# Rotated attention: masking by GpSimd after the exponential, values in every other slot, one query and key product

## The reference, cut to what matters

```
x = wide attention(x)                       # 16 heads of 64
x = causal attention with slopes(x)         # then a mixture of experts
x = rotated attention(x)                    # this one; then a mixture of experts
x = grouped attention(x), recurrence, grouped attention

q = (x @ Wqa @ Wqb).reshape(b, s, 16, 8)    # rotated attention
kv = (x @ Wkva @ Wkvb).reshape(b, s, 4, 8, 2)
q, k = rope(q), rope(k)                     # r1 = x1*cos - x2*sin, r2 = x1*sin + x2*cos
scores = q k^T * 8**-0.5, causal            # -inf above the diagonal
out = softmax(scores) @ v @ Wout + bout
```

## Time and profile before

| quantity | value |
|---|---|
| median of 3 runs | 2320.3 us |
| the profiled execution, its own time | 2318.05 us |
| its span, first to last instruction | 2316.3 us |
| rotated attention, first to last `score` | 1388.6 to 1606.5 us |
| PE busy over the span | 88% |
| DVE, ACT, POOL busy over the span | 67%, 52%, 36% |
| mean granted TensorE clock | 0.933 |

### The profile page before, as it was taken

The page is one execution under the profiler, slowest core; times in us unless marked ns, Lnnn a source line. Parts: engine busy times, 40 slices in busy tenths (PEclk is TensorE's granted clock), DMA queues, the critical chain, the costliest instruction groups (busy, mean ns, idle before and its releaser), DMA issues. The chain is left out here.

```text
span 2316.3 us, 52936 instructions
## 1 busy us (share of the span) xinstructions
PE 2046.8 (88%) x20735; PEld 1381.6 (60%) x20735; DVE 1544.5 (67%) x2742; ACT 1199.4 (52%) x2044; POOL 826.4 (36%) x1272
## 2 busy tenths in 40 slices
PE   5999999999969997999779989997599995479996
PEld 3666666666657895566569976664355543335553
DVE  4777778787754444677354447775689875768993
ACT  3444444444343333666723326665478776447774
POOL 4444444444425341333044514441233323423330
PEclk9999999999969997999789999999699997669998
DMA  5000000000000021444000204441234420124441
GB/s 169 1 1 1 1 1 1 1 1 1 2 0 7 5 56 44 121 121 115 3 4 1 56 16 118 122 117 33 71 102 116 116 61 1 43 79 110 116 110 45
DMA packets 157124, 120.99 MB, mean 52 GB/s; under 512 B 13856, under 2 KB 129456, under 8 KB 156884
## 3 DMA queue, kind: packets, MB, share of 16 engines
q1 hardware_dynamic: 156884, 117.65, 18.8%
HBM read 63.48 MB, written 54.12 MB: 51 GB/s over the span
## 5 line engine op out<-in xcount | busy, mean ns | idle before, releaser
L911 DVE TENSOR_REDUCE l_group_mx<-maxima 128x4 f32<-128x1024 f32 x248 | 303.9, 1226 | 58.8 <-PE maxima L704 57.3
L839 ACT ACTIVATE l_group_pr<-scores 128x1024 f32<-128x1024 f32 x256 | 261.7, 1022 | 72.0 <-PE scores L725 69.4
L2176 POOL TENSOR_TENSOR l_wide_tiles_sum<-l_wide_pr 128x256 f32<-128x256 f32 x256 | 180.9, 728 | 212.2 <-ACT l_wide_pr L2119 212.2
L2147 DVE RECIPROCAL l_wide_rc<-bank 128x256 f32<-128x256 f32 x128 | 223.9, 1749 | 8.4 <-PE bank L2080 7.9
L2119 ACT ACTIVATE l_wide_pr<-scores 128x512 f32<-128x512 f32 x256 | 139.0, 595 | 163.1 <-PE scores L2063 163.1
L2131 DVE TENSOR_REDUCE l_wide_mx<-maxima 128x2 f32<-128x512 f32 x248 | 159.4, 685 | 52.9 <-PE maxima L2043 52.5
L2109 ACT ACTIVATE l_wide_qk<-bank 128x512 f32<-128x512 f32 x128 | 76.5, 597 | 175.6 <-PE bank L2030 175.6
L911 DVE TENSOR_REDUCE l_slope_mx<-maxima 128x6 f32<-128x768 f32 x124 | 118.9, 959 | 64.9 <-PE maxima L711 63.3
L911 DVE TENSOR_REDUCE l_rope_mx<-maxima 128x6 f32<-128x768 f32 x124 | 118.8, 958 | 44.0 <-PE maxima L711 43.0
L839 ACT ACTIVATE l_slope_pr<-scores 128x768 f32<-128x768 f32 x128 | 103.6, 810 | 77.6 <-PE scores L732 77.4
L745 PE MATMUL bank<-l_group_pr,va 128*32 128x256 f32 x2048 | 143.4, 399 | 0.0
(11 more groups left out here) (468 smaller groups left out, 4852.3 us busy)
## 6 DMA issues: line engine op xcount, KB each, us to landing
l_group_st<-stack_dram SPq DMA_DIRECT2D x128, 192.0 KB, 3.8
l_slope_st<-stack_dram SPq DMA_DIRECT2D x64, 192.0 KB, 3.8
l_rope_st<-stack_dram SPq DMA_DIRECT2D x64, 192.0 KB, 3.9
stack_dram<-l_group_parts SPq DMA_DIRECT2D x64, 192.0 KB, 2.3
stack_dram<-l_group_parts SPq DMA_DIRECT2D x64, 128.0 KB, 1.9
stack_dram<-l_slope_parts SPq DMA_DIRECT2D x32, 192.0 KB, 2.4
stack_dram<-l_rope_parts SPq DMA_DIRECT2D x32, 192.0 KB, 2.3
stack_dram<-l_slope_parts SPq DMA_DIRECT2D x32, 128.0 KB, 2.2
```

The costliest lines, as they stand in the source:

```text
L839: act.activation(pr[:, i % AHEAD, :, 0:keys], Tp[:, :, 0:keys], ACT.Exp).then_inc(s["exps"], 1)
L911: dve.tensor_reduce(mx[:, b % 2, :, :, i], max_bank(i, b)[:, :, 0:BLOCKS * keys].rearrange("p z (a k) -> p z a k", k=keys), AX.X, ALU.max, ...
L2147: own.done(dve.reciprocal(rc[:], Ob[i % 2][:, S:2 * S]))
L2176: pool.tensor_tensor(tiles_sum[:, i % 2, z, :], pr[:, i % 2, z, 0:S], pr[:, i % 2, z, S:2 * S], ALU.add).then_inc(s["added"], 1)
```

## The change

Only "rope" computes differently; of the other kinds one table entry is written in another form.

1. The corner matmuls of `score` (L732) are left out for "rope". Instead POOL zeroes the exponentials above the diagonal in place with one `affine_select` per pair, a new piece `cut`. `value i` waits for the cuts of its two pairs, no longer for the exponentials.
2. `swapped` is gone, with its weights. `by_sin` is made from the same product as `by_cos`: DVE reads partitions 64 to 127 and writes 0 to 63, and the other way round, in two instructions of 64 partitions. The sine table is exchanged to match.
3. `parts` is divided into three pieces, with a `cut` between them. In "slope" and "group" the three stand one behind the other, as before.
4. The slots of "rope" are set anew on all engines. `value` stands in slots 1, 3, 5 and 7 of PE (before 1, 2, 5, 6), `qk` in slot 2 together with `v`, `turnmax` in slot 4 (before 3). `max` is one slot later against `score`.

```diff
     "rope": {
         "pe": [
-            [("score", 2, 0), ("max", 7, 1), ("qk", 0, 3), ("value", 0, 0)],
+            [("score", 2, 0), ("max", 6, 1), ("qk", 0, 3), ("v", 0, 2)],
...
         "pool": [
-            [("split", 0, 1)],
-            [("parts", 0, 3)],
+            [("split", 0, 1), ("cut", 3, 0), ("parts", 0, 3)],
+            [("cut", 4, 0), ("parts", 1, 3)],
...
     "rope": {
-        "pe": [("norm", 0, 0), ("norm", 0, 1), ("qk", 0, 0), ("swapped", 0, 0), ("qk", 0, 1), ("swapped", 0, 1), ("v", 0, 0), ("v", 0, 1)],
+        "pe": [("norm", 0, 0), ("norm", 0, 1), ("qk", 0, 0), ("qk", 0, 1), ("v", 0, 0), ("v", 0, 1)],
...
-                if causal:
+                if kind == "slope":
                     for half in range(2):
...
-                pe.wait_ge(s["exps"], PAIRS * b + 2 * i + 2)
+                pe.wait_ge(s["cut"] if kind == "rope" else s["exps"], PAIRS * b + 2 * i + 2)
...
-                dve.tensor_tensor(by_cos[:], bank[:].rearrange("p (a s) -> p a s", a=2),
-                                  angles[:, 0, :].unsqueeze(1).to_broadcast([P, 2, S]), ALU.mult).then_inc(drained[m], 1)
-            elif what == "swapped":
-                if b == 0:
-                    dve.wait_ge(s["set_act"], 2)
-                wait(dve, s["summed"], b)
-                dve.tensor_tensor(by_sin[:], bank[:].rearrange("p (a s) -> p a s", a=2),
-                                  angles[:, 1, :].unsqueeze(1).to_broadcast([P, 2, S]), ALU.mult).then_inc(drained[m], 1)
+                both = bank[:].rearrange("p (a s) -> p a s", a=2)
+                dve.tensor_tensor(by_cos[:], both, angles[:, 0, :].unsqueeze(1).to_broadcast([P, 2, S]), ALU.mult)
+                for z in range(2):
+
+                    mine, other = slice(64 * z, 64 * z + 64), slice(64 * (1 - z), 64 * (1 - z) + 64)
+                    ins = dve.tensor_tensor(by_sin[mine], both[other], angles[other, 1, :].unsqueeze(1).to_broadcast([64, 2, S]), ALU.mult)
+                ins.then_inc(drained[m], 1)
...
+            elif what == "cut":
+                pool.wait_ge(s["exps"], PAIRS * b + i + 1)
+                own_tiles = pr[:, i % AHEAD].rearrange("p z (t q) -> p z t q", q=S)[:, :, :, 0:P]
+                pool.affine_select(out=own_tiles, in_=own_tiles, compare_op=ALU.is_ge, fill=0.0, base=0,
+                                   pattern=[[0, 2], [0, NT], [1, P]], channel_multiplier=-1).then_inc(s["cut"], 1)
```

More of the change, by code:

```diff
@@ L251 @@
     "slope": {"norm": 1, "qk": 0, "turnmax": 0, "turn1": 1, "v": 0, "turn0": 0},
-    "rope": {"norm": 1, "qk": 0, "swapped": 1, "turnmax": 0, "turn1": 1, "attn": 1, "v": 0, "project": 1, "turn0": 0},
+    "rope": {"turn0": 0, "project": 1, "qk": 0, "v": 1, "turn1": 0, "turnmax": 1, "attn": 0, "norm": 1},
     "group": {"norm": 0, "qk": 1, "turnmax": 1, "turn1": 0, "reg_scores": 1, "attn": 0, "v": 1, "project": 1, "reg_turn": 0, "turn0": 1, "reg_value": 0},
@@ L309 @@
         "pe": [
-            [("score", 0, 0), ("max", 5, 1), ("swapped", 0, 3)],
-            [("score", 1, 0), ("max", 6, 1), ("value", 3, -1)],
-            [("score", 2, 0), ("max", 7, 1), ("qk", 0, 3), ("value", 0, 0)],
-            [("score", 3, 0), ("max", 0, 2), ("turn1", 0, -1), ("turnmax", 0, 1)],
-            [("score", 4, 0), ("max", 1, 2), ("v", 0, 2), ("attn", 0, -1)],
-            [("score", 5, 0), ("max", 2, 2), ("value", 1, 0)],
-            [("score", 6, 0), ("max", 3, 2), ("project", 0, -1), ("value", 2, 0)],
@@ L317 @@
-            [("score", 7, 0), ("max", 4, 2), ("turn0", 0, 0), ("norm", 0, 4)],
+            [("score", 0, 0), ("max", 4, 1), ("turn0", 0, -1), ("project", 0, -2)],
+            [("score", 1, 0), ("max", 5, 1), ("value", 3, -1)],
+            [("score", 2, 0), ("max", 6, 1), ("qk", 0, 3), ("v", 0, 2)],
+            [("score", 3, 0), ("max", 7, 1), ("value", 0, 0)],
+            [("score", 4, 0), ("max", 0, 2), ("turn1", 0, -1), ("turnmax", 0, 1)],
+            [("score", 5, 0), ("max", 1, 2), ("value", 1, 0)],
@@ L318 @@
+            [("score", 6, 0), ("max", 2, 2), ("attn", 0, -1), ("norm", 0, 4)],
+            [("score", 7, 0), ("max", 3, 2), ("value", 2, 0)],
         ],
         "act": [
-            [("norm", 0, 3), ("score", 0, 0)],
-            [("score", 1, 0), ("xn", 0, 4)],
+            [("score", 0, 0)],
+            [("score", 1, 0)],
             [("take", 1, -1), ("score", 2, 0)],
-            [("score", 3, 0)],
-            [("score", 4, 0)],
-            [("attn", 0, -1), ("score", 5, 0)],
-            [("take", 0, 0), ("v", 0, 2), ("score", 6, 0)],
@@ L327 @@
-            [("score", 7, 0)],
+            [("score", 3, 0), ("v", 0, 2)],
+            [("score", 4, 0), ("xn", 0, 5)],
+            [("score", 5, 0)],
+            [("take", 0, 0), ("score", 6, 0)],
+            [("score", 7, 0), ("attn", 0, -1), ("norm", 0, 4)],
         ],
         "dve": [
-            [("turn0", 0, -1), ("max", 5, 1)],
-            [("swapped", 0, 3), ("max", 6, 1)],
-            [("max", 7, 1), ("join", 0, 1), ("qk", 0, 3)],
-            [("max", 0, 2)],
+            [("max", 4, 1)],
@@ L334 @@
+            [("turn0", 0, -1), ("project", 0, -2), ("max", 5, 1)],
+            [("max", 6, 1)],
+            [("qk", 0, 3), ("max", 7, 1)],
+            [("join", 0, 1), ("max", 0, 2)],
             [("turnmax", 0, 1), ("turn1", 0, -1), ("max", 1, 2)],
             [("max", 2, 2)],
-            [("max", 3, 2), ("project", 0, -1)],
-            [("max", 4, 2)],
+            [("max", 3, 2)],
         ],
         "pool": [
-            [],
-            [],
-            [("split", 0, 1)],
-            [("parts", 0, 3)],
@@ L440 @@
 for _kind in FIRST:
-    FIRST[_kind]["pool"] = [("parts", 0, 0), ("parts", 0, 1)]
+    FIRST[_kind]["pool"] = [("parts", _i, _b) for _b in range(HOSTED) for _i in range(3)]
     FIRST[_kind]["sp"] = [(_what, _i, _b) for _b in range(HOSTED) for _what, _i in (
@@ L551, in bank_of @@
         def bank_of(what, b):
-            early = causal and b < HOSTED and what in ("norm", "qk", "swapped", "v")
+            early = causal and b < HOSTED and what in ("norm", "qk", "v")
             return (Ob if early else Mb)[fill[what, b][0]]
@@ L672, in pe_piece @@
                 ins.then_inc(full[m], 1)
-            elif what in ("qk", "swapped"):
-                if what == "qk" and b == 0:
+            elif what == "qk":
+                if b == 0:
                     pe.wait_ge(s["weights"], 1)
@@ L1082, in host @@
             if what == "first":
-                first(engine, eng)
+                first(engine, eng, 3 if engine == "pool" else 1)
             elif what in ("stat0", "stat1"):
```

63 lines of the change are left out of this document (32 added, 31 removed).

## The result

The changed kernel took 2353.27 us (median of 4 runs, 2351.68 to 2359.26), the kernel before on the same chip 2318.35 (4 runs, 2312.38 to 2320.38): ratio 1.0164, 95% interval 1.0142 to 1.0186. The forecast was 2344, range 2323 to 2368. The profiled span grew from 2316.3 to 2352.3.

A forecast was written before the change was run, and what follows sets the result against it. Waits for DVE's reads and POOL's cuts, not PE, were to bound a batch: 16.0 us for 13.92. Eleven full distances (+23), the ends and -2.1 in the experts gave +26.5, less 1: 2344 us, range 2323 to 2368.

The forecast's parts named there:

- PE stops being the bound: Rotated attention: 2.2 to 2.4 us a batch leave PE, but waits for DVE and POOL make it 16.0 for 13.92.
- Rival 1: Every rope batch: PE stays the bound, DVE's reads hidden, rounds closing in 1.51 us; -29 us, 2289 us; chance 10%.
- DVE's waits: Longer DVE work between reductions starts `max 6` 0.7 us late, `max 0` about 1.0, `turnmax` 0.6.
- The reads: DVE's three reads of the product, 0.61 + 0.61 + 0.62 = 1.84 us in one piece ahead of pair 7's reduction.
- POOL's queue and the cut: Behind `split`, cuts of 0.66 us and pieces of `parts` end at 15.2; `value 2` waits 1.5 us for cut 5.
- Rival 3: POOL's select as dear as a subtraction, 1.16 us a cut: batch 17.8, about 2368 us; chance 12%.
- rival 2: POOL reaches cut 5 early, cuts cost nothing on the path: +0.9 to +1.6 us a batch, 2329 to 2338; chance 17%.
- `spread` half a microsecond behind: The `spread` DMA, behind `high`, is usable at 15.5 us of the 16.0 batch; cheaper cuts win only that half.
- The ends: First `score 0` +0.9 us, first two distances +2.6, last two +0.8, behind the last `score 0` +1.3.
- "11 x 2.1" term: Eleven full distances from `score 0` to `score 0`, each 16.0 us for 13.92, together +23 us.

The follow-up runs named there:

- e2: Changed kernel with the two sine reads of 64 partitions made one of 128, leaving out the exchange of halves; 2342.50 us, ratio 1.0111.
- e9: Kernel before with only the single product and its three reads; corner matmuls kept, no cuts, order and banks of before; 2322.42 us, ratio 1.0034.
- e7: Changed kernel with cut 5 moved ahead of piece 1 of the parts in GpSimd's lists; 2338.57 us, ratio 1.0102.
- e11: Changed kernel with cuts of half the width, the second 64 queries of each diagonal tile left uncut; 2338.19 us, ratio 1.0108.
- e1: Changed kernel without cuts on GpSimd, corner matmuls back in the score, values waiting for the exponentials; 2335.22 us, ratio 1.0078.
- e4: Changed kernel with v and norm moved into PE's waits and repeated three and five times there; 2355.04 us, ratio 1.0169.

## Why the prediction was right, and where its size was off

**PE stops being the bound.** Right: busy 12.35 of 16.36, before 13.92 of 13.92. Rival 1 needed VectorE's reads hidden in the 0.55 us gaps; the waits for L909 are all there.

**DVE's waits.** `max 0` 1.29 late (forecast 1.0), `max 6` 0.53 (0.7), `turnmax` 0.37 (0.6). The reads were the mis-sized term: 2.13 us from 1494.40 to 1496.53, forecast 1.84. The working took 0.61 for a 0.69 us instruction, as the next one starts before the end of the last. For full reads that is right: in e2 they start 0.61 apart. The three of the change start 0.71 apart, so the overlap is lost there. The same happens in e9, which has these reads in another order; only the reads that go from one half of the partitions to the other differ from e2's. The 0.29 is most of the 0.36 us by which the batch at full clock is over 16.0; POOL's queue has 0.13, and small gains go the other way. That a read of 64 partitions costs as much as one of 128 held.

**POOL's queue and the cut.** Right in order, place and size. e7 and e11 show it twice over: moving the cut removes the wait of `value 2`, and shortening it brings PE's waits for cuts from 9.5 us to 1.7. (The forecast's 3.4 us for every 0.08 us of a cut is too much by its own sum: three cuts in eleven batches give 2.6.) Rival 3 (1.16 us a cut) and rival 2 (cuts free) fall with it. Rival 2's own figure of 2329 to 2338 is about where e7 and e11 end, since both take the cut off the path and meet the next wait.

**`spread` half a microsecond behind.** Right, and it needed e1 and e7 to be seen: in both `score 0` waits for it, up to 1.4 and 1.3 us, once the cuts are out of the way.

**The ends.** First `score 0` not late at all (forecast +0.9), and the first two distances +5.4 instead of +2.6. The first distance alone is 17.97 for 15.00, and the clock has a part in it: it was still at its lower level for most of that batch, with a mean of 0.57, where the kernel before had 0.88.

```profile
1385.71:1403.68 17.97, 15.07 (x157) 8.89 (x158) 10.84 (x14) 8.38 (x14) 9.68 (x16) 0.57 0.36 93
```

How large that part is wasn't separated. The tail was 2.0 us shorter than reckoned. These nearly cancel, and that is luck. Each kernel has one profile, and what follows the stage, unchanged in all of them, took between 649 and 657 us from the first `max` of "group" on, so a microsecond or two at the ends can be chance.

**The clock.** The step that failed. The forecast expected the granted clock to stay at 2.4 GHz, because "no idle time is over 1.5 us". (Nor had it survived "waits of 0.2 us only": the kernel before kept 1.00 through waits of 0.6 and 0.4.) It fell in nearly every batch. A batch that lost nothing by it, and two stretches at the lower level in the batch of 17.82:

```profile
1437.80:1454.16 16.36, 13.46 (x191) 9.13 (x188) 11.73 (x20) 8.90 (x15) 11.15 (x19) 0.90 0.37 101
1448.80:1452.30 3.50, 3.50 (x38) 2.11 (x32) 1.98 (x3) 1.77 (x3) 3.37 (x5) 0.51 0.34 97
1471.16:1476.20 5.04, 5.04 (x52) 3.57 (x48) 3.38 (x7) 1.62 (x2) 2.70 (x5) 0.50 0.48 141
1482.90:1486.40 3.50, 3.50 (x43) 2.04 (x42) 1.75 (x5) 1.81 (x3) 3.44 (x5) 0.51 0.14 37
```

```profile
1453.37 0.86 PE L745 MATMUL bank<-l_rope_pr,va 128*32 128x256 f32 x16 [0.68 <-POOL l_rope_pr L1025]
...
1488.19 0.86 PE L745 MATMUL bank<-l_rope_pr,va 128*32 128x256 f32 x16 [0.37 <-POOL l_rope_pr L1025]
```

A mean near 0.50 is the 1.2 GHz level, where the value pair takes 1.51 us for 0.86. What a fall costs depends on where it lies. From 1448.80 and from 1482.90 it lies late in the batch, ahead of `value 2`. POOL's queue doesn't slow down with PE, so `value 2` only waits less, 0.68 and 0.37 us instead of 1.53, and the time of the batch is still set by cut 5: such a fall alone costs nothing (16.36).

A fall that covers the first microseconds of a batch, as from 1471.16, delays the product, the reads and `split`, and so the cuts: `split` starts 1.46 us later into the batch than at full clock (1481.40 against 1497.76), which is the whole of 17.82 against 16.36. A fall over `value 2` itself makes it 17.0.

Seven of the eleven full distances are longer than 16.41 by falls at such places. Eleven at 16.36 would be 26.7 us over before; measured are 34.2, so 7.4 go with the clock. With 3.7 from the batch's own 0.36 that is the whole miss of the "11 x 2.1" term. The attribution to the clock rests on neighbouring batches with the same instructions; no edit held the clock up throughout.

The forecast said that a fall would put the time above the range; it put it 9 us above the forecast and inside. That statement was wrong too, as it hadn't been priced, and that the falls often lay where they cost nothing was luck.

The Trainium skill, TensorE: Matmul & The Clock Gate, Part 1, has the full clock given by recent activity and not by default. The rows agree in kind: it was never lost in the batches of before that had PE busy 13.92 of 13.92, and it was lost in batches with waits. Why e4 lost it from one batch to the next they don't tell.
